# Spreading the expert weight preparation over the batch loop, reordering the first loads, and merging instructions of the routed stage of a two-layer attention and mixture-of-experts kernel

## What is computed

```
layer 0: causal softmax attention with 16-wide q and k over x itself; then x @ ternary(W).T * scale
layer 1: per token a structural-similarity score of q and k, a small conv "ODE" over the 512 tokens,
         sigmoid, softmax over tokens, times v * channel gate, projected
         out_low = weights[..., None] * v * ch_w ;  return out_low @ proj_w + proj_b
         then a mixture of experts: layer norm h, one shared expert for every token and the best of 8
         routed experts times its gate, silu(h @ W1q.T) @ W2q.T
         w_q = clip(round(W / mean|W|), -1, 1) * mean|W|     (per row of W; "ternary map")
```

## Time and profile before

| | |
|---|---|
| runs | 909.64, 910.66, 913.33 us |
| profiled execution | 912.14 us, of which the span is 910.8 us |
| granted TensorE clock, mean | 0.956 |
| PE busy / DVE / ACT / POOL | 782.4 (86%) / 727.4 (80%) / 698.1 (77%) / 315.1 us (35%) |
| moved by DMA | 80.81 MB, mean 89 GB/s |

### The profile page before, as it was taken

The page is one execution under the profiler, slowest core; times in us unless marked ns, Lnnn a source line. Parts: engine busy times, 40 slices in busy tenths (PEclk is TensorE's granted clock), DMA queues, the critical chain, the costliest instruction groups (busy, mean ns, idle before and its releaser), DMA issues. The chain is left out here.

```text
span 910.8 us, 18608 instructions
## 1 busy us (share of the span) xinstructions
PE 782.4 (86%) x5514; PEld 621.8 (68%) x5514; DVE 727.4 (80%) x2321; ACT 698.1 (77%) x1561; POOL 315.1 (35%) x384
## 2 busy tenths in 40 slices
PE   0568899999999999999999999988757878888783
PEld 0346678778878878878878877866435767767672
DVE  1777999778878878888887887977563889989995
ACT  0447887688697697697697797786746989999995
POOL 2000001012422323323333323434561555556556
PEclk9976999999999999999999999999887999999997
DMA  7132331110221211201203201101127775445441
GB/s 201 60 116 92 124 122 57 47 49 24 82 67 40 76 54 52 82 19 65 83 18 111 82 20 41 37 30 48 47 83 218 181 203 164 151 146 167 130 106 56
DMA packets 50979, 80.81 MB, mean 89 GB/s; under 512 B 8954, under 2 KB 27838, under 8 KB 50880
## 3 DMA queue, kind: packets, MB, share of 16 engines
q1 hardware_dynamic: 39056, 53.46, 20.7%
q0 software_dynamic: 9984, 25.29, 7.7%
q10 hardware_dynamic: 1840, 0.86, 0.3%
HBM read 49.57 MB, written 32.11 MB: 90 GB/s over the span
## 5 line engine op out<-in xcount | busy, mean ns | idle before, releaser
L3621 POOL DMA_INDIRECT out<-G_y,Gid x80 | 83.1, 1039 | 77.8 <-ACT G_y L1867 56.1
L1220 PE MATMUL bank<-E2T,G_Sh 128*128 (+1 forms) x320 | 74.3, 278 | 39.7 <-DVE G_Sl L3426 39.6
L3493 POOL DMA_INDIRECT rrec<-R,pos x64 | 64.3, 1005 | 82.0 <-DVE R L2111 67.2
L1849 ACT ACTIVATE G_S<-bank,e1b,e1s 128x256 f32<-128x256 f32 x160 | 91.6, 693 | 0.0
L519 PE MATMUL bank<-X,PT 128*128 128x257 f32 x320 | 82.5, 392 | 2.5 <-DVE X L1954 1.3
L3484 POOL DMA_INDIRECT hrec<-HN,pos x64 | 65.3, 1020 | 52.0 <-DVE pos L2234 37.2
L3452 POOL TENSOR_TENSOR R<-rstd,mhalf 128x4 f32<-128x4 f32 x16 | 17.4, 1089 | 184.2 <-DVE rstd L1910 184.2
L1208 PE MATMUL bank<-G_T,E1T 128*128 128x256 f16 x640 | 80.0, 280 | 1.0 <-DVE G_T L3417 1.0
L3460 POOL TENSOR_TENSOR R<-V,mhalf 128x8 f32<-128x8 f32 x16 | 26.7, 1666 | 142.7 <-DVE V L1920 142.7
L1220 PE MATMUL bank<-E2T,G_Sl 128*128 (+1 forms) x320 | 74.6, 278 | 0.0
L1208 PEld LDWEIGHTS bank<-G_T,E1T 128*128 (+1 forms) x640 | 64.4, 101 | 9.7 <-issue 1.4
(11 more groups left out here) (362 smaller groups left out, 2597.5 us busy)
## 6 DMA issues: line engine op xcount, KB each, us to landing
G_r<-rrec SPq DMA_DIRECT2D x40, 258.0 KB
G_h<-hrec SPq DMA_DIRECT2D x40, 257.0 KB, 2.8
X<-in_x SPq DMA_DIRECT2D x16, 512.0 KB, 5.2
XT<-in_xT SPq DMA_DIRECT2D x16, 512.0 KB, 4.3
e1n<-in_ew SPq DMA_DIRECT2D x8, 512.0 KB, 3.4
e2n<-in_ew SPq DMA_DIRECT2D x8, 512.0 KB, 3.4
rrec<-rpad SPq DMA_DIRECT2D x18, 129.0 KB, 4.9
hrec<-hpad SPq DMA_DIRECT2D x18, 128.5 KB, 4.7
```

The source lines that it names most:

```text
L1220: last = pe.matmul(banks[j][:, 0:D], x[w % NGB][:, f, j * P:(j + 1) * P], E2T[:, expert_of[w], f, :], start=k == 0, stop=k == 2 * FC - 1)
L1849: act.activation(G_S[w % 2][:, ff, :], bk[:, (ff - f0) * SLOT:(ff - f0 + 1) * SLOT], ACT.Silu, bias=e1b[:, expert_of[w], ff], scale=e1s[:, ...
L3493: pool.indirect_dma_start(rrec[:], bass.IndirectOffsetOnAxis(pos[b % 2][:, j:j + 1], 0), R[b % 2][:, j, :], None).then_inc(s[f"rrec{b % 2} ...
L3621: pool.indirect_dma_start(t["out"], bass.IndirectOffsetOnAxis(Gid[w % 6][:, j:j + 1], 0), G_y[w % 3][:, j, :], None, bounds_check=TOK - 1, ...
```

## The change

1. Maps: only the shared expert and expert 7 stay in the prologue. The other seven are made one per turn of the pair loop (6) and in the tail (1). Their transposes and scale matmuls go through bank 2 (shared with `ode`) in place of 6 and 7; rank and place move from bank 2 to bank 6. e1n, e2n, the f16 results and dg share one 4 KB region, so the loads of one expert follow each other: e2n waits for et0, the next e1n for et1 and dgm.
2. guard runs twice, once for the shared expert (in the prologue) and once for the 8 routed ones (in the tail), with own `sdn`/`sup` columns.
3. First loads: XT(0), e1n, X(0), e2n lead SyncE's queue behind wqk; w0, wall and three weights go on ScalarE's; the small ones come later and in two groups (`small`, `tiny`).
4. gamma goes into the stored row: new GpSimd step `hg` per batch multiplies 128x1024 f32 in place, between the transposes hT and the scatters hsc, which wait for it.
5. Routed stage: gT, gTl, gSh and gSl are single instructions, gT and gTl without the scale; ge2 is gone and gy reads `e2s` at a register's place. Rings: G_h, G_r 5, G_T, G_Sh, G_Sl, G_y 4, G_S 3, Gid 8. The order of each engine's loop is new.
6. All lists of the front are put in another order.

```diff
-NGR, NGB = 4, 3
+NGR, NGB, NGS, NGY, NGI = 5, 4, 3, 4, 8
...
+        def load_e1(q):
+            if q == 1:
+                sp.wait_ge(s["et0"], 1)
+            elif q >= 2:
+                sp.wait_ge(s["et1"], q)
+                sp.wait_ge(s["dgm"], q)
+            sp.dma_start(e1n[:], w.rearrange("(c p) n -> p c n", p=P)).then_inc(s["e0n"], 16)
...
+        def load_e2(q):
             if q >= 1:
+                sp.wait_ge(s["et0"], q + 1)
...
+        load_xT(0)
+        load_e1(0)
+        load_x(0)
+        load_e2(0)
+        load_xT(1)
+        load_small()
+        load_x(1)
+        load_e1(1)
+        load_tiny()
...
         for g in range(2, 8):
+            load_x(2 * g)
+            load_xT(2 * g)
+            load_x(2 * g + 1)
+            one_e2(g - 2)
+            load_xT(2 * g + 1)
+            one_e1(g - 1)
...
-        for w in range(48):
-            rload(w - 8)
-            gload(w - 3)
-            pads(w - 4)
+        for w in range(46):
+            gload(w - 1)
+            pads(w - 5)
+            rload(w - 2)
...
         def nb(g):
             if g >= 1:
-                pe.wait_ge(s["place"], at("place", GB * g - 1, 0))
+                pe.wait_ge(s["e2s"], g + 2)
...
         def up(b, f):
             elif f == 1:
-                pe.wait_ge(s["rout"], at("rout", b, 0))
+                pe.wait_ge(s["place"], at("place", b, 0))
...
-            o, tile = banks[2][:, 0:NT * NE], lambda j: OH[:, b * NT + j, :]
+            o, tile = banks[6][:, 0:NT * NE], lambda j: OH[:, b * NT + j, :]
...
PE order, start:
-        w0sum()
-        proj(0)
-        w0T()
+        proj(0)
+        w0sum()
+        map_et0(0)
         for i in range(4):
             score(0, i)
...
PE order, loop over pairs:
+            one_et0(g - 2)
             dqk(2 * g - 2, 1)
             dqk(2 * g - 2, 2)
+            dqk(2 * g - 2, 3)
+            fuse(2 * g - 2)
...
+            u(2 * g - 2, 1)
+            one_et1(g - 2)
...
             ffn(2 * g - 1, 0)
+            one_dg(g - 2)
...
DVE order, loop: one1(g - 2, 0..5) between qks(2g-2, 2) and x3(2g-3, 1); one0(g - 1, 0..6) from acc(2g-4) on
...
         def gT(w):
-            for c in range(DC):
-                act.activation(G_T[w % NGB][:, 0, c, :], banks[6 + w % 2][:, c * SLOT:(c + 1) * SLOT], ACT.Copy,
-                               scale=gamc[:, c:c + 1]).then_inc(s["gT"], 1)
+            act.activation(G_T[w % NGB][:, 0].rearrange("p c n -> p (c n)"), banks[6 + w % 2][:], ACT.Copy).then_inc(s["gT"], 1)
...
-        def gSh(w, i):
-            act.activation(G_Sh[w % NGB][:, f0:f0 + 2], G_S[w % 2][:, f0:f0 + 2], ACT.Copy, scale=sdn[:]).then_inc(s["gSh"], 1)
+        def gSh(w):
+            act.activation(G_Sh[w % NGB][:], G_S[w % NGS][:], ACT.Copy, scale=sdn[:, 1:2]).then_inc(s["gSh"], 1)
...
-        for w in range(48):
-            gsilu(w - 4, 0)
-            gT(w - 2)
-            gn(w - 7, 0)
-            gSh(w - 4, 0)
-            gsilu(w - 4, 1)
-            ge2(w - 3)
-            gn(w - 7, 1)
-            gSh(w - 4, 1)
+        for w in range(46):
+            gT(w)
+            gn(w - 6, 0)
+            gSh(w - 3)
+            gn(w - 6, 1)
+            gsilu(w - 2, 0)
+            gsilu(w - 2, 1)
...
+            dve.tensor_tensor(G_T[w % NGB][:, 1].rearrange("p c n -> p (c n)"), banks[6 + w % 2][:],
+                              G_T[w % NGB][:, 0].rearrange("p c n -> p (c n)"), ALU.subtract).then_inc(s["gTl"], 1)
...
+            dve.scalar_tensor_tensor(G_Sl[w % NGB][:], G_S[w % NGS][:], sdn[:, 1:2], G_Sh[w % NGB][:], ALU.mult, ALU.subtract).then_inc(s["gSl"], 1)
...
+        def hg(b):
+            pool.wait_ge(s["hT"], at("hT", b, 1))
+            h = HN[b % 2][:, :, 0:D]
+            pool.tensor_tensor(h, h, gamx[:, None, :].to_broadcast([P, NT, D]), ALU.mult).then_inc(s["hg"], 1)
...
         def hsc(b, j):
             if j == 0:
                 pool.wait_ge(s["place"], at("place", b, 2))
-                pool.wait_ge(s["hn"], at("hn", b, NT - 1))
+                pool.wait_ge(s["hg"], at("hg", b))
```

More of the change, by code:

```diff
@@ L253, in program @@
     front_end = here[0]
-    here[0] = late_end
+    here[0] = front
     q_n = sb("q_n", [P, NE])
@@ L840, in pe_program @@
         pv(0, 1)
-        map_et0(0)
         pv(0, 2)
@@ L866, in pe_program @@
-        map_dg(2)
-        map_et1(2)
-        pv(1, 3)
-        x2T(0, 0)
-        map_et0(3)
-        x2T(0, 1)
-        map_dg(3)
-        proj(2)
+        score(1, 2)
+        map_et0(1)
+        score(1, 3)
+        ffn(0, 0)
+        nmrow(1)
+        ffn(0, 1)
+        scoreT(1, 0)
+        ffn(0, 2)
+        scoreT(1, 1)
+        scoreT(1, 2)
+        ffn(0, 3)
+        scoreT(1, 3)
+        for i in range(4):
+            pv(1, i)
+        x2T(0, 0)
+        proj(2)
+        x2T(0, 1)
@@ L874, in pe_program @@
+        map_et1(1)
+        gate1(0)
         dqk(0, 0)
-        gate1(0)
-        map_et1(3)
-        gate2(0)
+        x1T(1, 0)
         score(2, 0)
         score(2, 1)
-        x1T(1, 0)
+        gate2(0)
+        for i in range(1, 4):
+            dqk(0, i)
+        fuse(0)
         score(2, 2)
-        map_et0(4)
-        map_et1(4)
+        x1T(1, 1)
+        guard_max(0)
+        map_dg(1)
         score(2, 3)
-        x1T(1, 1)
-        dqk(0, 1)
+        u(0, 0)
+        ffn(1, 0)
         nmrow(2)
-        ffn(1, 0)
+        u(0, 1)
@@ L2752, in dve_program @@
+        ode(0, 1)
+        x2(2, 1)
+        for i in range(2, 5):
+            ode(0, i)
+        one0(0, 3)
+        Ml_(1)
+        ve0(2)
+        x2p(0, 3)
+        x2(2, 2)
+        x2p(1, 0)
+        for i in range(5, 8):
+            ode(0, i)
+        guard(0, 5)
+        one0(0, 4)
+        x2p(1, 1)
         x2(2, 3)
+        rinv(3, 0)
+        x2p(1, 2)
+        x1(3, 0)
         ode(0, 8)
-        map0(8, 5)
+        ve1(2)
         ode(0, 9)
-        map1(8, 3)
-        ode(0, 10)
@@ new lines, in dve_program @@
+            if g == 8:
+                guard(1, 9)
+            ode(g - 1, 4)
+            if g == 0:
+                map1(1, 0)
+                map1(1, 1)
+            if g == 9:
+                sort(7)
+            for i in range(5, 8):
+                ode(g - 1, i)
+            if g == 9:
+                sort(8)
+            if g == 0:
+                map1(1, 2)
+            x2(2 * g, 1)
+            router(2 * g - 3, 6)
+            y(2 * g - 3, 0)
+            ode(g - 1, 8)
+            ode(g - 1, 9)
@@ L3215, in dve_program @@
+        router(12, 0)
+        x3(13, 3)
+        for i in range(1, 4):
+            router(12, i)
+        ve2(13)
         router(12, 4)
         router(12, 5)
+        ve0(15)
+        place(12, 0)
+        guard(1, 1)
+        x2p(14, 0)
+        guard(1, 2)
+        x2(15, 2)
+        x2(15, 3)
+        Sl_(12, 0)
+        rs3(12)
+        one0(7, 0)
+        Sl_(12, 1)
+        x2p(14, 1)
+        place(12, 1)
+        guard(1, 3)
+        ve1(15)
         Sl_(12, 2)
+        Sl_(12, 3)
+        r(11, 2)
```

2677 lines of the change are left out of this document (1297 added, 1380 removed), and 2 rows, old and new, of the table names.

## The result

The changed kernel took 922.19 us (median of 20 runs, 911.83 to 936.29) where the kernel before took 910.4 in its 20 runs beside it: ratio 1.0096, 95% interval 1.0069 to 1.0122. The ratio leaves out the four of the 20 runs that lie over 1.5% above the shortest, so it is smaller than that of the two medians (1.013). The kernel is 1% slower. The forecast was 873 us, 852 to 893. The profiled execution is the shortest of the 20 (911.83, span 910.5), as long as the profiled one of before, and far from it inside. First the busy time by stretch, cut as the earlier trace rows are: first proj to second, second to fifth, one pair of batches, the tail, the pads' stretch, 40 us of the steady routed stage.

What follows compares the result with a forecast made beforehand. PE was taken to bound the pair loop, with ACT busy throughout the routed stage. From 912.1 us, -13 -7 -11 +8.4 +3 -2 -18 +2 = -37.6 gave 874.5, less 1.5: 873 us, range 852 to 893.

Steps and rivals of the forecast that it cites:

- hg on GpSimd: Front stage: the gamma product takes 2 us on GpSimd, two a pair covered by its idle time, so no cost there.
- Rival (c): Pair loop: hg stops VectorE instructions with two SBUF tensors; 885 us at the upper price, nothing at 2 us; chance 0.08.
- Pair loop: Six maps return where PE is full, 1.4 us each, +8.4; half a microsecond a pair of stalls, +3.
- (e): Front: each map a serial chain of about 17 us on PE's queue; 921 us at half uncovered; chance 0.06.
- Tail: End of the front: eighth map and second guard fit 28 us of idle PE; -2 altogether, bounds -6 to +5.
- Routed stage: Period per block falls to 4.45 us, 5.15 where the pads go; -18 over 39 blocks.
- Rival (a): Routed stage keeps its pace, near 4.9 us, if merged instructions save nothing and gathers hold; 889 us; chance 0.14.
- Fill: Routed stage's start: rload(0) waits for the last residual scatter, single gSh and gSl lengthen a block's chain; +2.
- first loads: Start of the kernel: XT(0) behind wqk alone, the first maximum at 19.5 in place of 32.79; -13.
- the maps between second and fifth proj: Prologue: seven maps (9.8 us of PE) and most tiny bias matmuls (1.6) leave, PE's share counted whole; -11.
- (b): Prologue: a denser PE may escape the low clock, 14 us more gain, 859 us; chance 0.14.

Runs made afterwards that it cites:

- e9: e6 with GpSimd copying a block's ids two blocks earlier, ahead of the power; 910.88 us.
- e12: The changed kernel with hg on VectorE in place of GpSimd, behind the position cast of the same batch; 927.15 us.
- e14: The changed kernel without hg, the same kernel as e1 on another chip; 888.79 us, ratio to before 0.9783.
- e1: The changed kernel without hg (stored rows not multiplied by gamma and its scale); 892.1 us, ratio to before 0.9799.
- e2: The changed kernel with maps 2 to 8 in a block of their own ahead of the pair loop, hg kept; 1046.32 us.
- e18: The changed kernel itself, run again on the chip of e9 to e12; 931.37 us.
- e13: The changed kernel itself, run again beside e14, e15 and e16 on one chip; 918.11 us, ratio to before 1.0106.
- e7: e6 with gSl moved behind gy, gy0 and gy1 in VectorE's routed order; 893.17 us, ratio to before 0.9813.
- e16: The kernel of e11 again, on the chip of e13 to e15; 874.38 us, ratio to before 0.9637.
- e5: The changed kernel without hg, the scale by gamma put back into gT and gTl; 892.46 us, ratio to before 0.9786.
- e6: e5 with rload two blocks later in SyncE's order; 886.69 us, ratio to before 0.9732.
- e8: The kernel before with only the new order of the first loads; 896.93 us, ratio to before 0.9845.
- e4: The kernel before with a GpSimd multiply by ones of hg's size and place put in; 919.9 us, ratio to before 1.0109.
- e11: e9 with VectorE also making the variances ahead of gTl, so the power moves out of gSl; 908.81 us.
- e15: The kernel of e6 again, beside e16 on one chip; 885.04 us, ratio to before 0.9751.

## Why the prediction was wrong

**The failed step** is "hg on GpSimd", with the words "POOL has 22.9 of 69.7 busy, so two a pair are covered". The duration was right (2206 ns for 2). The cover was read on the wrong engine: on GpSimd hg was hidden, but it holds a DVE instruction for the whole 2.2 us. Rival (c) had this, for instructions with two SBUF tensors, and priced it by sums, and by them it costs nothing at 2 us. A sum tells whether a queue overflows, not who stands behind the held instruction. There it was Sl and HT, which PE's next step waits for. Measured: 29.3 us in all, 24.6 of them placed in the pairs and the tail, 3.8 to 4.6 a pair; on the chip of e9 to e12, where other waits stand in the pair, 0.7. Without hg the kernel takes 888.8 us (e14) and 892.1 (e1), which is inside the stated range, at its upper end.

**Pair loop.** PE's 1.4 a map became 2.2 measured (70.98 to 73.19), and the new order costs 1.3 by itself, for which my half microsecond of stall stood: +3.5 a pair for a predicted +1.9. The forecast's "PE still full" held only without hg. (e) is refuted twice: no wait for `eq`, E1T or e2s among PE's, and a tenth of the chain uncovered.

**Tail.** Predicted -2, measured +15.7 in the profiled execution: the map 4 to 8 and hg 6 to 10, the new order 1.3. My error was to count idle PE time (28 us) as room. A tail of chains has idle engines and no room; a map alone is a chain of 20.5 us (e2).

**Routed stage.** The instructions came as priced: gT 596 ns of busy time and gSh 1143 by their groups, from start to start in a full queue 0.48 (815.76 to 816.24) and 1.04 (811.83 to 812.87), for the 0.57 and 0.95 taken. The period did not follow, 4.71 to 4.93 a block (this profile, e18 and e13, counted as for e7; 5.07 before) in place of 4.45, since it was not ScalarE's queue but waits that set it: ACT is at 37.01 of 40. One of them I had only as a coupling of the two queues, GpSimd's power: it starts inside gSl and is held by it. The timeline of the profile after, DVE and POOL:

```profile
813.57 1.28 DVE L3444 SCALAR_TENSOR_TENSOR G_Sl<-G_S,sdn,G_Sh 128x1024 f16<-128x1024 f32 x1
813.74 1.69 POOL L3652 TENSOR_TENSOR rstd<-rstd,mhalf 128x2 f32<-128x2 f32 x1
...
815.47 0.16 DVE L3431 SCALAR_TENSOR_TENSOR gnb<-mv,rstd 128x2 f32<-128x2 f32 x1 [0.22 <-POOL rstd L3652]
```

The other is the gather of G_h behind the ids. With both moved (e16) the period is 4.65 and both queues are full; 0.2 over the 4.45, with the second gT and gTl, some 0.2 us of work in each, back in it. Rival (a) was half right in its time. Of its two reasons the gathers did hold the stage; that the merged instructions save nothing was wrong.

**Fill.** Predicted +2, measured +6.9; some 5 of it is rload(0) on SyncE (e5 to e6, 26.7 to 21.9).

**Right:** the first proj near 8 (7.84) and the second near 37 (38.10), the 13 us of the first loads (e8). The prologue was too low: -11 for the maps between second and fifth proj became 106.1 - 78.5 = -27.6. PE's busy time fell by 22.4 there, twice what my instructions make, and the granted clock rose from 0.87 to 0.93, which is (b) in part. But the clock isn't what shortened the stretch. It differs between executions of one front while the length hardly does: 0.83 and 107.0 us in e4, 0.87 and 106.1 in the profile before; 0.91 and 79.0 in e14, 0.94 and 78.9 in e1, 0.93 and 78.5 in the profile after. e8, with all maps in place, has 0.92 and 104.5. So (b)'s 14 us aren't in it. What fell most is VectorE's work, from 93.2 to 60.2 us, and I had counted PE's share alone (9.8 and 1.6 for -11). That VectorE's queue set this stretch is argued from these sums; no run takes the maps' VectorE work out by itself.

## What to carry to other kernels

An operation that moves to GpSimd isn't free because GpSimd is idle: look at which VectorE instruction it will lie beside (in this case one that read only SBUF was held and one that read a bank was not), and who waits behind that one, and price it there. Idle time in a stretch of chains is no room. When a merge or a ring is meant to shorten a period, first ask whether the queue is what sets it; here reordered steps (the ids and the power, e15 to e16, 10.7 us; rload, e5 to e6, 5.8) were worth more than the merged gT and gTl, and most of the change's loss was one helper instruction per batch.

## What the runs showed of the hardware

GpSimd and VectorE can hold each other for a whole instruction, both ways; in the rows here only where VectorE's instruction reads nothing but SBUF. A 128x1024 product on GpSimd (2.2 us) made a 128x4 cast on VectorE take 2.70 us in place of 0.17. VectorE's gSl (1.28 us, two SBUF tensors read) made a 128x2 power take 1.5 to 1.7 us in place of 0.75. In e16, where gSl no longer meets the power, it meets the next thing on GpSimd, and a copy of 128x2, 176 ns in e15, takes 1.1 us. POOL's groups of e16, 800 to 840:

```profile
L3648 POOL COPY Gid<-G_h 128x2 int32<-128x2 int32 x9 | 9.9, 1099 | 0.0
L3655 POOL TENSOR_TENSOR rstd<-rstd,mhalf 128x2 f32<-128x2 f32 x8 | 6.0, 748 | 0.1
```

The Trainium skill, SBUF — State Buffer, section "SBUF: two separate sides", says that the port pair the two share is an exclusive lock, taken for a whole instruction by whichever comes first, and that on VectorE's side it concerns instructions in one of its 2-port modes or with two inputs in SBUF. The trace agrees: the residual add and gSl have two such inputs, while instructions that read a bank and one tensor in SBUF run beside hg at their usual 0.74 us (e4, and HT in the profile after). The cast has one input, so by the page it would have been in a 2-port mode, which no trace shows. The trace adds that the size of the held instruction doesn't matter. In the rows the cast begins 0.5 us before hg and is held all the same, so their order can't be read off the starts.

The second surprise is the chip on which PE's releases come up to 3.9 us late (e9 to e11). The kernel before lost little by it (its median there was 915.27 and 911.39, elsewhere 908.75 to 911.13), while the front of e6 and e9, the same code, went from 73.2 to 79.2 us a pair. Why it happens is open.
